# Sixteen dense experts on one Trainium2 core: the token's share multiplied into the hidden values, one PSUM accumulation over all experts

## The reference

```python
logits = hidden_states @ router_w + router_b
probs = jax.nn.softmax(logits, axis=-1)
topw, topi = jax.lax.top_k(probs, K)                 # K = 4 of E = 16
topw = topw / jnp.sum(topw, axis=-1, keepdims=True)
combine = jnp.sum(jax.nn.one_hot(topi, E) * topw[..., None], axis=2)
def body(acc, expert):                               # for each of the 16 experts
    hmid = jax.nn.gelu(x @ w1e + b1e, approximate=False)     # 128 -> 256
    return (acc + (hmid @ w2e + b2e) * ce[:, None], None)    # 256 -> 128, ce = the token's share
```

## Time and profile before

| | us |
|---|---|
| median of 3 runs | 1095.7 (1094.6 to 1095.91) |
| the profiled execution's own time | 1094.63 |
| its span | 1092.9 |
| PE, DVE, ACT, POOL busy over the span | 955.5, 773.3, 639.5, 488.2 |
| first mixture, from its first DVE work to its last | 258.3 to 489.9 |
| PE's granted clock over the whole span | 0.93 |

### The profile page before, as it was taken

The page is one execution under the profiler, slowest core; times in us unless marked ns, Lnnn a source line. Parts: engine busy times, 40 slices in busy tenths (PEclk is TensorE's granted clock), DMA queues, the critical chain, the costliest instruction groups (busy, mean ns, idle before and its releaser), DMA issues. The chain is left out here.

```text
span 1092.9 us, 20105 instructions
## 1 busy us (share of the span) xinstructions
PE 955.5 (87%) x6024; PEld 605.4 (55%) x6024; DVE 773.3 (71%) x2421; ACT 639.5 (59%) x1418; POOL 488.2 (45%) x590
## 2 busy tenths in 40 slices
PE   2999999985999999987999899999999998960696
PEld 1444444433788888873445565556555655650585
DVE  4567677725898989887889888879887987443121
ACT  1366565642777777763566657665767566730253
POOL 4132332212122222211466867686668668924155
PEclk9999999955899999997999999999999988975798
DMA  3000000004400000000000000000000000005730
GB/s 89 1 2 1 1 1 1 2 1 152 110 29 20 19 19 19 10 1 1 1 1 1 1 2 1 1 2 1 2 1 2 1 1 1 1 1 191 230 119 14
DMA packets 23415, 28.80 MB, mean 26 GB/s; under 512 B 3340, under 2 KB 19729, under 8 KB 23328
## 3 DMA queue, kind: packets, MB, share of 16 engines
q1 hardware_dynamic: 21168, 24.53, 7.3%
q0 software_dynamic: 1728, 3.17, 0.8%
q10 hardware_dynamic: 432, 0.01, 0.0%
HBM read 20.57 MB, written 8.04 MB: 26 GB/s over the span
## 5 line engine op out<-in xcount | busy, mean ns | idle before, releaser
L1114 POOL TENSOR_SCALAR probs<-probs,rinv 128x128 f32<-128x128 f32 (+3 forms) x256 | 274.4, 1087 | 122.6 <-DVE rinv L990 122.6
L1058 ACT ACTIVATE pt<-psum 128x128 f32<-128x128 f32 (+3 forms) x256 | 98.4, 434 | 110.3 <-PE psum L863 109.1
L1049 ACT ACTIVATE probs<-probs,rowmin 128x128 f32<-128x128 f32 (+3 forms) x256 | 141.4, 558 | 32.6 <-DVE rowmin L984 31.3
L984 DVE CUSTOM_DVE_ANT_0 probs<-psum,adj 128x128 f32<-128x128 f32 (+3 forms) x256 | 122.1, 477 | 43.1 <-PE psum L853 26.4
L535 ACT ACTIVATE pT<-psum 128x1024 f32<-128x1024 f32 (+3 forms) x128 | 89.9, 702 | 69.0 <-PE psum L365 67.4
L853 PE MATMUL psum<-k_sb,q_sb 64*128 64x256 f32 (+3 forms) x512 | 113.2, 495 | 16.7 <-DVE rowmin L984 16.2
L474 DVE TENSOR_REDUCE top<-psum 128x2 f32<-128x256 f32 (+3 forms) x128 | 101.7, 817 | 24.8 <-PE psum L353 24.6
L973 DVE MAX8 top<-w 128x8 f32<-128x131 f32 (+3 forms) x208 | 103.2, 496 | 4.6
L1458 ACT ACTIVATE m_hid<-psum,b1t 128x512 f32<-128x512 f32 x128 | 88.2, 689 | 24.2 <-DVE m_hid_lo L1332 21.9
L863 PEld LDWEIGHTS psum<-ident,probs 128*128 128x128 f32 x640 | 68.7, 142 | 59.6 <-POOL probs L1114 32.2
L863 PE MATMUL psum<-ident,probs 128*128 128x128 f32 x640 | 100.1, 288 | 0.7 <-POOL probs L1114 0.7
(11 more groups left out here) (242 smaller groups left out, 1941.9 us busy)
## 6 DMA issues: line engine op xcount, KB each, us to landing
s_wb<-in_w_all SPq DMA_DIRECT2D x15, 514.5 KB
sorted_x<-blank SPq DMA_DIRECT2D x1, 3870.0 KB, 19.8
s_xg<-sorted_x SPq DMA_DIRECT2D x15, 258.0 KB, 5.6
m_w1s<-in_w SPq DMA_DIRECT2D x16, 128.0 KB, 2.1
m_w2s<-in_w SPq DMA_DIRECT2D x16, 128.0 KB, 2.1
x_tok<-in_x SPq DMA_DIRECT2D x4, 256.0 KB, 4.0
bv<-in_b_v SPq DMA_DIRECT2D x1, 512.0 KB, 4.9
wq<-in_wq SPq DMA_DIRECT2D x1, 512.0 KB, 4.5
```

Of the source, the lines that this page charges most:

```text
L984: dve.tensor_tensor_reduce(probs[:, k, 0:K], s_bank[h][:, 0:K], adj[:, OFF[i]:OFF[i] + K], 1.0, FLOOR, ALU.add, ALU.min, rowmin[:, k:k + 1 ...
L1049: act.activation(probs[:, k, 0:K], probs[:, k, 0:K], ACT.Exp, bias=rowmin[:, k:k + 1], scale=-1.0, accum_out=rsum[:, k:k + 1]).then_inc(ex ...
L1058: act.activation(pt[:, (2 * n + h) % 4, 0:K], t_bank[h][:, 0:K], ACT.Copy).then_inc(pt_ready, 1)
L1114: pool.tensor_scalar(probs[:, k, 0:K], probs[:, k, 0:K], rinv[:, k:k + 1], None, ALU.mult).then_inc(normed, 1)
```

## The change: what it does

The share is multiplied into the hidden values ahead of the second product: gelu(x W1 + b1) * share. With that, all 16 experts add up in PSUM: `pe_second` writes the bank of its chunk (`o_bank` now has four banks), starts at expert 0 and stops at expert 15. `act_out`, `pe_back` and `dve_acc` of each unit are gone; at the end four copies to `y`, 16 transposes and four additions to `x_tok` remain. The b2 term is one matmul for each chunk (`pe_bias`, 16 partitions, b2 by the shares) during expert 1.

Since tokens are columns there, the shares are needed as rows repeated over all 128 partitions. PE transposes `comb`, ACT copies it (`act_comb`), SP stores it to a DRAM tensor `shares` and loads it back broadcast over the partitions, for two experts at a time at the start and then 1 MB for each following expert inside SP's loop.

The rounding is no longer by a second Gelu or DVE copy: DVE multiplies both halves in one instruction (`dve_scale`), ACT rounds both in one Copy (`act_round`), DVE subtracts both in one instruction (`dve_low`). The router now runs for each chunk apart, inside the front's loop. One step of each engine is now: PE first(n+2), second(n); DVE low(n+1), scale(n+2); ACT round(n+1), hidden(n+2). In SP's list the stores and broadcast loads stand ahead of attention 1's weights and the fill of `sorted_x`.

```diff
+                def later(e, u, k, by):
+                    return (e, u, k + by) if k + by < CH else (e + 1, 1 - u, k + by - CH)
...
                     for f in range(NF):
-                        pe.wait_ge(hid_read, LEAD + j - 3)
+                        pe.wait_ge(hid_full, LEAD + j - 3)
...
                 def pe_second(pe, e, u, k):
-                    pe.wait_ge(lo_ready, LEAD + (n + 1) * NF)
-                    pe.wait_ge(y_ready, LEAD + n - 1)
+                    pe.wait_ge(lo_ready, LEAD + e * CH + k + 1)
                     for f in range(NF):
-                        pe.matmul(dst, w2_hi[:, u, f, :], hid_hi[:, k % HB, f, :], start=(f == 0), stop=False)
+                        pe.matmul(o_bank[k][:], w2_hi[:, u, f, :], hid_hi[:, k % HB, f, :], start=first and f == 0,
+                                  stop=False, skip_group_check=True)
...
+                def pe_bias(pe, k):
+                    if k == 0:
+                        pe.wait_ge(comb_back, 32)
+                    pe.matmul(o_bank[k][:], b2_e[:], comb_e[:, k, :], start=False, stop=False, skip_group_check=True)
...
+                    for k in range(LOOK):
+                        pe_first(pe, 0, 0, k)
+                    for q in range(CH):
+                        pe.wait_ge(comb_ready, q + 1)
+                        pe.transpose(o_bank[q][0:E * TC, 0:P], comb[:, q, :, :].rearrange("p e t -> p (e t)"),
+                                     ident[:]).then_inc(comb_turned, 1)
...
+                def dve_scale(dve, e, u, k, t):
+                    n = e * CH + k
+                    if k == 0:
+                        dve.wait_ge(share_in[u], 16 * CH + 16 * t)
+                    dve.wait_ge(hid_full, LEAD + (n + 1) * NF)
+                    h = hid[:, k % HB, :, :]
+                    dve.tensor_tensor(h, h, share[:, u, k, :].unsqueeze(1).to_broadcast([P, NF, 512]),
+                                      ALU.mult).then_inc(scaled, 1)
                 def dve_low(dve, e, u, k):
+                    dve.wait_ge(rounded, n + 1)
+                    dve.tensor_tensor(hid_lo[:, k % HB, :, :], hid[:, k % HB, :, :],
+                                      hid_hi[:, k % HB, :, :].bitcast(F32), ALU.subtract).then_inc(lo_ready, 1)
                 def dve_pair(dve, t, last):
-                                dve_low(dve, *later(e, u, k))
-                                dve_acc(dve, *before(e, k))
+                            if k + 1 < CH or u == 0 or not last:
+                                dve_low(dve, *later(e, u, k, 1))
+                            if k + LOOK < CH or u == 0 or not last:
+                                e2, u2, k2 = later(e, u, k, LOOK)
+                                dve_scale(dve, e2, u2, k2, t if u == 0 or k + LOOK < CH else t + 1)
...
+                    dve_scale(dve, 0, 0, 0, 0)
+                    dve_low(dve, 0, 0, 0)
+                    dve_scale(dve, 0, 0, 1, 0)
...
                 def act_hidden(act, e, u, k):
                         act.wait_ge(hidden, j + 1)
-                        act.wait_ge(lo_ready, LEAD + (n + 1 - HB) * NF)
+                        if f == 0:
+                            act.wait_ge(lo_ready, LEAD + n + 1 - HB)
                         apart(act, passed)
+                        act.activation(hid[:, k % HB, f, :], h_bank[(k * NF + f) % 4][:], ACT.Gelu,
+                                       bias=b1t0[:, bass.ds(e * NF + f, 1)]).then_inc(hid_full, 1)
+                def act_round(act, e, u, k):
+                    act.wait_ge(scaled, n + 1)
+                    act.wait_ge(expert_out, LEAD + n + 1 - HB)
                     apart(act, passed)
+                    act.activation(hid_hi[:, k % HB, :, :], hid[:, k % HB, :, :], ACT.Copy).then_inc(rounded, 1)
                 def act_pair(act, t, last):
+                            if k + 1 < CH or u == 0 or not last:
+                                act_round(act, *later(e, u, k, 1))
                             if k + LOOK < CH or u == 0 or not last:
-                                act_hidden(act, *later(e, u, k))
-                            act_out(act, e, k)
+                                act_hidden(act, *later(e, u, k, LOOK))
...
+                    act_hidden(act, 0, 0, 0)
+                    act_comb(act, 0)
+                    act_comb(act, 1)
+                    act_hidden(act, 0, 0, 1)
+                    act_comb(act, 2)
+                    act_comb(act, 3)
+                    act_round(act, 0, 0, 0)
...
+                def sp_program(sp):
...
+                    for q in range(CH):
+                        sp.wait_ge(comb_copied, q + 1)
+                        sp.dma_start(shares[q].rearrange("e (t p) -> (e t) p", p=P), comb_t[:, q, :]).then_inc(comb_stored, 16)
+                        sp.wait_ge(comb_stored, 16 * (q + 1))
+                        for u in range(2):
+                            sp.dma_start(share[:, u, q, :], shares[q, u].partition_broadcast(P)).then_inc(share_in[u], 16)
+                    sp.dma_start(comb_e[:], shares[:, :, :].rearrange("q e n -> e q n")).then_inc(comb_back, 16)
+                    load_attention(sp, 1)
...
+                            sp.wait_ge(scaled, (t * 2 + u + 1) * CH)
+                            sp.dma_start(share[:, u, :, :], shares[:, e, :].rearrange("q e n -> (q e) n").partition_broadcast(P)).then_inc(share_in[u], 16)
```

More of the change, by code:

```diff
@@ L1158, in experts0 @@
             E, I, TOPK = E0, I0, 4
-            rw, b1t, b2t, func = rw0, b1t0, b2t0, ACT.Gelu
             NF = I // P
             HB = 4
-            LOOK = HB // 2
-            PADW = 8 - TOPK
-            RW = E + PADW
+            LOOK = 2
+            RW = E + 8 - TOPK
             CH = T * P // 512
             TC = T // CH
+            UNITS = E * CH
             w1d, w2d = a["w1_0"], a["w2_0"]
@@ L1222, in experts0 @@
                 y_back = s_("y_back")
-                acc = s_("acc")
                 h_bank = banks[0:4]
-                o_bank = banks[4:6]
-                back_bank = banks[6:8]
-                def act_rounds(f):
-                    return f % 2 == 0
-                ROUND_D = sum(not act_rounds(f) for f in range(NF))
+                o_bank = banks[4:8]
+                def later(e, u, k, by):
+                    return (e, u, k + by) if k + by < CH else (e + 1, 1 - u, k + by - CH)
                 def pe_first(pe, e, u, k):
@@ new lines, in pe_second, with pe_back @@
+                        mm = pe.matmul(o_bank[k][:], w2_hi[:, u, f, :], hid_lo[:, k % HB, f, :], start=False,
+                                       stop=last and f == NF - 1, skip_group_check=True)
+                    mm.then_inc(expert_out, 1)
+                def pe_bias(pe, k):
+                    if k == 0:
+                        pe.wait_ge(comb_back, 32)
+                    pe.matmul(o_bank[k][:], b2_e[:], comb_e[:, k, :], start=False, stop=False, skip_group_check=True)
+                def pe_back(pe, k):
+                    pe.wait_ge(y_ready, k + 1)
+                    if k == 0:
+                        pe.wait_ge(hid_full, LEAD + UNITS * NF)
@@ L1284, in pe_pair @@
                             if k + LOOK < CH or u == 0 or not last:
-                                pe_first(pe, *later(e, u, k))
+                                pe_first(pe, *later(e, u, k, LOOK))
                             pe_second(pe, e, u, k)
-                            if k or u or not isinstance(t, int) or t:
-                                pe_back(pe, *before(e, k))
-                    if last:
-                        pe_back(pe, e, CH - 1)
+                            if isinstance(t, int) and t == 0 and u == 1:
+                                pe_bias(pe, k)
                 def pe_program(pe):
-                    lead(pe, (expert_out, y_back))
+                    lead(pe, (expert_out,))
                     for q in range(CH + 1):
@@ L1392, in dve_program @@
                 def dve_program(dve):
-                    lead(dve, (lo_ready, acc))
+                    lead(dve, (lo_ready,))
                     c = Steps(0, 2 * T + CH)
-                    for q in range(CH + 2):
+                    step = Steps(0, CH * (10 + 2 * TC))
+                    for q in range(CH + 3):
                         if q < CH:
@@ L1399, in dve_program @@
                             dve_norm(dve, c, q - 1)
-                        if q >= 2:
+                        if 2 <= q <= CH + 1:
                             dve_split(dve, q - 2)
+                            dve_logits(dve, step, q - 2)
+                        if q >= 3:
+                            dve_route(dve, step, q - 3)
                     c.close()
-                    step = Steps(0, 11 + 2 * T)
-                    dve.wait_ge(logits, 1)
-                    lp = banks[5][:, 0:T * E].rearrange("p (t e) -> p t e", e=E)
@@ L1429, in dve_program @@
-                    dve.wait_ge(router_step, step.done())
-                    for k in range(LOOK):
```

(12 more changed lines are left out.)

219 lines of the change are left out of this document (98 added, 121 removed).

## The result

The changed kernel takes 1168.4 us (median of 4, 1167.3 to 1170.7) against 1095.2 for the kernel before (median of 4): ratio 1.068, interval 1.065 to 1.071. Forecast were 1160 and a range of 1130 to 1190. The profiled execution took 1167.3, with a span of 1165.5: 72.6 us above that of before.

A forecast was written before the change was run, and what follows sets the result against it. PE bound the old loop; a ring between ACT and DVE would bound the new. First 311.0, plus 62 periods (238.7) and 6.1 at the end gave 555.8, 65.9 us later than before: 1160, range 1130 to 1190.

The forecast's parts named there:

- the ring: In the expert loop, ACT's round and Gelus and DVE's scale wait in turn: 3.85 us a unit; chance 0.80.
- PE: In the loop, the transposes leave PE: 0.46 us a unit, 29 us in all if PE remained the bound.
- The members of the ring: Per unit: R (ACT round) 1.02, H (Gelus) 1.26, C (DVE scale), L (DVE low) 1.21 each; period without POOL 3.65 us.
- POOL: In the loop, POOL's weight split slows DVE's two-input operations: about 0.84 us an expert, 0.21 a unit.
- The loop: Over the experts' units: 62 periods of 3.85 us, 238.7 us, ending at 549.7.
- The front: Before the loop, router and share round trips make the first second product start at 309.8, 24 us later.
- Moved past in SP's list: Expert 2's weights, behind the fill, land at 327 to 331 with 3 us of cover; if gone, at most some 5.
- The end: After the loop's last period, 6.1 us to the last addition, so the stage ends at 555.8.
- A sign that was off: PE would be idle over a quarter of the loop.
- B (PE as the bound): In the loop, PE stays the bound at 2.78 us a unit: 1091, or 1082 with a shorter front; chance 0.06.
- C (the clock): In the loop, PE's idle time drops its clock to 1.2 GHz: 1238, or about 1200 half the time; chance 0.10.
- D (share loads of 1 MB): In the loop, share loads over 15 us hold up the multiplication: 1225 at 20 us an expert; chance 0.04.

The follow-up runs named there:

- e4_twice: The changed kernel with ACT's round done twice in each unit, once more into a spare tile: 1224.1 us, ratio 1.118.
- e2_act: The changed kernel with only ACT's order turned (hidden ahead of round), DVE's left: 1172.2 us, ratio 1.073.
- e3_dve: The changed kernel with only DVE's order turned (scale ahead of low), ACT's left: 1159.7 us, ratio 1.056.
- e1_both: The changed kernel with both orders turned (ACT hidden ahead of round, DVE scale ahead of low): 1138.7 us, ratio 1.039.
- e11_again: e10_split with the fill first, expert 0's shares awaited by chunk and two chunks' shares transposed and copied before the first Gelu, in more rounds: 1088.0 us, ratio 0.9915.
- e5_fill: The changed kernel with attention 1's weight loads and the fill of sorted_x put back ahead of the shares' stores and loads: 1162.7 us, ratio 1.061.
- e12_nopool: The changed kernel with POOL's weight split left out for experts 2 to 15, which use the first two's split weights: 1153.0 us, ratio 1.052.
- e10_split: e9_look3 with the first product's weights split once their last first product has run, each product waiting for its own weights: 1112.3 us, ratio 1.011.
- e9_look3: e1_both with LOOK = 3 instead of 2, all engines one unit further ahead of the second product: 1175.9 us, ratio 1.072.

## Why the prediction was right

The forecast was the ring, and the ring it is. That isn't only argued from the waits: lengthening one member by a copy lengthened every unit (e4_twice), turning one order left a ring of the same length (e2_act, e3_dve), turning both made the unit shorter (e1_both). Its steps, with the stage's end at 555.8 forecast and 563.0 measured:

- *PE.* The transposes went, 0.46 us a unit forecast. The price is right: 2.76 us a unit in e11_again. It could not be collected while PE was not the bound.
- *The members of the ring.* Forecast R 1.02, H 1.26, C and L 1.21, period without POOL 3.65. Measured 1.06, 1.25, 1.23 and 1.23, period 3.61; the next ACT instruction starts 0.10 ahead of the end of the one before, and C also 0.08 ahead of L's end (421.96 against 422.04).
- *POOL.* Forecast 0.84 us an expert, on the ring; measured 0.76 in the timeline and 0.7 between e5_fill and e12_nopool. The size is near, but by luck: the prediction took it from a slowing of both sides, and the traces show that one side waits for the other. Alone, L and C take 1.23 us, and POOL's L1526 and L1528 take 0.40 and 0.74. One that starts more than 0.14 us before the end of the other engine's ends 1.09 (L, C), 0.26 (L1526) or 0.60 us (L1528) behind the end of that other, its own duration less 0.14. L1528 of POOL ends at 425.13, and L ends 1.09 later, at 426.22; L1526 of POOL ends 0.26 behind L, at 426.48; C 1.07 behind that, at 427.55; L1528 of POOL 0.61 behind C, at 428.16. All 32 such instructions of the changed kernel between 345 and 470 us end within 0.02 us of this. The Trainium skill, "SBUF — State Buffer", section "Who interferes with whom", has the two instructions exclude each other, as the prediction read it; here the trace agrees. The 16 us more that the prediction worked out beside it didn't come, since not all four instructions of POOL hold up the ring: the first (423.92) falls into DVE's idle time, the second holds up L by 0.56, the third holds up C by 0.18, and the third and fourth wait for DVE themselves.
- *The loop.* 3.79 against 3.85: 62 x 0.06 = 3.7 us less than forecast.
- *The front.* C(1) ended at 315.0, not 311.0. The router was done at 294.6 (forecast about 294) and SP's first store went out at 291.6 (291.8). What was missed is the later rounds: 4.3 us, not 3.0. From the issue at 294.29 to that of the loads at 297.82 it was 3.5 us, where 2.1 was taken for a store. That store stands behind two loads of 256 KB that were issued in the 0.8 us before it. The first store had none ahead of it and was waited for 1.9 us (291.56 to 293.42), so the loads ahead are the likely cause; no run sets them apart.
- *Moved past in SP's list.* The term that failed most. Forecast was a cover of 3 us for expert 2's weights, and no cost. The fill took 25.1 us to land, not 19.8, and held SP for 13.6 us, not 10.4; not shown, but likely, is that this was because attention's weights and the last shares, issued in the 3.4 us before it, were still under way. The weights landed at 335.8 instead of 327 to 331, and it cost some 6 us (e5_fill). The prediction's "at most some 5 us" had the mechanism.
- *The end.* 7.1 us from the last C to the last addition, not 6.1. The prediction let the bank of the last chunk alone be late. But all sixteen transposes stand behind the last second product in PE's list, so the additions of the other three banks are late as well: four additions of 0.62 at the end, not one.
- *A sign that was off.* PE was to be idle over a quarter of the loop; by the profile it was idle for 42 of 215 us, a fifth. PE's 2.76 us of work in a period of 3.79 leave 1.03, but the last matmul of a group is shown with 0.39 us, longer than the 0.23 from one start to the next.

The terms add up: +4.0 (front) +6 (late weights) -3.7 (period) +1.0 (end) = 7.3, against 563.0 - 555.8 = 7.2. So the forecast of 1160 was 8 us low, mostly by transfers behind transfers.

*The rivals.* B (PE as the bound) was wrong for this kernel, and e10_split shows what it asked for: both orders, a third unit of look-ahead and a split in two pieces. C (the clock) didn't happen: granted 1.00 from 350 us to the end of the loop, with PE idle for 42 of 215 us. D (share loads of 1 MB) didn't either: 8.6 us to landing (median) out of 15.2 for an expert, and no C but the first waited for a transfer by the trace.

## What to carry to other kernels

Before you trust the sums of busy time, write down each engine's list for two neighbouring units and follow the waits until one comes back to where it began: the length of such a ring, divided by the units it spans, is a bound like an engine's busy time. When you take one ring apart, look for the one that the new order makes, over all engines and over two units. Here the turned orders made a ring through PE (e1_both), and the longer look-ahead made PE wait for the weight split (e9_look3). The loop reached PE's bound only when all of these were gone (e10_split), and the kernel beat the one before only with the front mended too (e11_again). Where two engines exclude each other, ask which of them starts first and what it holds up, not only how long both work. And a transfer's landing time holds for the queue it was read on: a store and its wait took 3.5 us behind 512 KB of loads where 2.1 was read, and 128 KB of weights took 13.1 us (median of three) around the fill of 3.9 MB.

## What the runs showed of the hardware

*With a like share of idle time, but in longer pieces, the clock fell.* In the changed kernel PE waited 0.55 to 1.15 us in each unit between 365 and 550 us, and the granted clock was 1.00 from 350 us on. In e9_look3 it waited 3.0 us once an expert, 27.1 of 155 us. The windows of that kernel around one such wait:

```profile
474.00:476.00 2.00, 2.00 (x10) 1.64 (x9) 1.72 (x3) 1.42 (x4) 1.92 (x2) 1.00 0.00 0
476.00:478.00 2.00, 0.41 (x2) 0.00 (x0) 2.00 (x2) 0.87 (x1) 1.75 (x3) 1.00 0.00 0
478.00:480.00 2.00, 0.57 (x1) 0.50 (x2) 0.69 (x1) 0.00 (x0) 1.27 (x1) 0.63 0.37 128
480.00:482.00 2.00, 2.00 (x6) 1.61 (x5) 0.00 (x0) 0.65 (x1) 0.00 (x0) 0.50 0.71 158
```

The clock fell to 0.50 (1.2 GHz) during the wait (0.52 between 478.5 and 479; PE came back at 479.43) and stayed there until about 485, at 6 matmuls in 2 us instead of 10. So the slow stretch came on top of the wait. It didn't follow every time: a wait of 3.0 us came nine times between 345 and 500 us, and behind two of them (ended at 384.68 and 414.93) the clock stayed at 1.00. Over 345 to 500 us the mean was 0.89. In e4_twice, where PE waited 1.70 us ahead of 502.06 and 2.15 ahead of 507.25, the mean from 345 to 520 us was 0.94; it fell to 0.60 behind the second of these waits and stayed at 1.00 behind the first. The Trainium skill, "TensorE: Matmul & The Clock Gate", section "A second HAM failure mode: psum-queue depth-cycling", warns of short idle times between groups of matmuls that make the clock swing: in these two kernels the trace agrees (0.89 and 0.94), in the changed one it doesn't (1.00). That the length of a single wait is what matters is a guess from these three kernels; no run varied it alone.

*DVE's two-input work and POOL's split exclude each other.* Whichever started first ran at its own length, and the other stood until it ended: L took 1.79 us instead of 1.23 behind a POOL instruction of 0.74, and POOL's L1528 took 1.60 instead of 0.74 behind C (426.56 above). So each side's loss depends on which one is first. The split of an expert's weights took 3.4 us before (386.91 to 390.28; one of its four instructions is in the earlier trace rows), and 5.5 us in e9_look3 (409.31 to 414.78), where its four instructions took 0.79, 1.60, 1.17 and 1.58 us instead of 0.40, 0.74, 0.40 and 0.74, and where it became what PE waited for.
